# Exponent rows of the next head pair made behind the eighth score product of a pair, their copy behind the seventh exponential

## The reference

```python
q = einsum('bfd,dnh->bfnh', layernorm(x), wq) * 8 ** -0.5      # 16 heads of 8, 128 queries
k = einsum('btd,dnh->btnh', ctx, wk); v = einsum('btd,dnh->btnh', ctx, wv)   # 2048 keys
w = softmax(einsum('btnh,bfnh->bnft', k, q) + bias)            # over the keys
x = x + einsum('bfnh,nhd->bfd', einsum('bnft,btnh->bfnh', w, v), wo)
```

## Time and profile before

| what | value |
|---|---|
| median of 3 runs | 306.6 us (306.28 to 307.88) |
| the profiled execution | 306.75 us, its span 304.7 us |
| PE busy | 280.7 us (92%) |
| DVE busy | 228.3 us (75%) |
| ACT busy | 205.3 us (67%) |
| POOL busy | 70.9 us (23%) |
| mean granted TensorE clock | 0.989 of full speed |

### The profile page before, as it was taken

How to read it: one execution, slowest core, us unless ns; L and a number is a source line. 1 busy time by engine, 2 the same in 40 slices (tenths; PEclk the granted TensorE clock), 3 DMA queues, 4 the chain that set the end, 5 groups by cost and what they waited for, 6 DMA issues and landing times.

```text
span 304.7 us, 10417 instructions
## 1 busy us (share of the span) xinstructions
PE 280.7 (92%) x4400; PEld 181.5 (60%) x4404; DVE 228.3 (75%) x376; ACT 205.3 (67%) x419; POOL 70.9 (23%) x140
## 2 busy tenths in 40 slices
PE   7956999999989999889999899999899999999995
PEld 6544666666656665453656566666656666436575
DVE  5954889999799994474478999999799970753583
ACT  4647688988878987623454888988788987133350
POOL 6694510110110121421022865010010030020001
PEclk9995999999999999999999999999999999999999
DMA  7974414532212380233200036322222100000000
GB/s 244 406 256 134 162 55 169 193 89 87 71 54 76 91 295 2 105 140 106 68 1 0 5 89 227 126 85 67 73 72 59 54 3 4 0 2 2 0 0 17
DMA packets 10897, 28.11 MB, mean 92 GB/s; under 512 B 2241, under 2 KB 3329, under 8 KB 10466
## 3 DMA queue, kind: packets, MB, share of 16 engines
q1 hardware_dynamic: 10776, 27.22, 27.1%
q10 hardware_dynamic: 74, 0.20, 0.2%
HBM read 20.79 MB, written 6.62 MB: 90 GB/s over the span
## 4 chain that ended last, share of the span: by engine, by line
PE 59%; DVE 25%; ACT 5%; issue 3%; POOL 3%; DMA 3%; ACTq 1%; POOLq 0%; DVEq 0%
PE bank L1099 58%; DVE mx L852 15%; ACT probs L573 2%; DMA k_first_rows<-kparts 2%; DVE o_rec L809 1%; DMA kpair<-k_first_rows 1%; POOL m_rows L444 1%; DVE negm L859 1%; POOL m_rows L446 1%; DVE kparts L821 1%; DVE k_rest L818 1%; DVE s_neg L911 1%; DVE xn L779 1%; DVE st L760 1%; ACT o_all L500 1%
## 5 line engine op out<-in xcount | busy, mean ns | idle before, releaser
L852 DVE TENSOR_REDUCE mx<-bank 128x2 f32<-128x1024 f32 x128 | 152.7, 1221 | 15.9 <-PE bank L1099 13.3
L573 ACT ACTIVATE probs<-bank 128x512 f32<-128x512 f32 x256 | 139.8, 596 | 18.4 <-PE bank L1099 13.7
L1099 PE MATMUL bank<-q_exp,kpair 64*128 64x128 bf16 x1024 | 87.1, 218 | 1.6 <-ACT probs L573 1.2
L1099 PE MATMUL bank<-probs,v_all 128*9 128x128 f32 x2048 | 79.9, 274 | 1.6 <-ACT probs L573 1.4
L1099 PE MATMUL bank<-kpair,q_rows 64*128 64x512 bf16 x256 | 72.8, 386 | 5.6 <-DMA kpair<-k_first_rows 4.4
L1099 PEld LDWEIGHTS bank<-q_exp,kpair 64*128 64x128 bf16 x1024 | 56.0, 94 | 33.0 <-ACT probs L573 13.6
L1099 PEld LDWEIGHTS bank<-probs,v_all 128*9 128x9 f32 x2048 | 43.4, 90 | 18.0 <-ACT probs L573 4.3
L444 POOL CAST m_rows<-negm 128x2 bf16<-128x2 f32 x32 | 7.1, 221 | 136.6 <-DVE negm L859 136.6
L1099 PEld LDWEIGHTS bank<-kpair,q_rows 64*128 64x128 bf16 x256 | 22.4, 93 | 8.0 <-issue 4.8
L500 ACT ACTIVATE v_all<-bank 128x512 f32<-128x512 f32 (+1 forms) x20 | 10.5, 538 | 14.2 <-PE bank L1099 14.2
L374 POOL TENSOR_TENSOR y<-ve,mhalf 128x1 f32<-128x1 f32 (+1 forms) x10 | 5.8, 581 | 50.8 <-DVE ve L766 50.8
(11 more groups left out here) (224 smaller groups left out, 339.9 us busy)
## 6 DMA issues: line engine op xcount, KB each, us to landing
k_scratch<-kparts SPq DMA_DIRECT2D x24, 256.0 KB, 2.9
kpair<-k_scratch SPq DMA_DIRECT2D x62, 96.0 KB
kpair<-k_scratch SPq DMA_DIRECT2D x62, 64.0 KB
ctxT_s<-in_ctxT SPq DMA_DIRECT2D x4, 512.0 KB, 6.3
mask_s<-in_mask SPq DMA_DIRECT2D x2, 1024.0 KB, 11.2
kpair<-k_scratch SPq DMA_DIRECT2D x62, 32.0 KB
wM<-in_packM SPq DMA_DIRECT2D x1, 1728.0 KB, 7.1
wB<-in_packB SPq DMA_DIRECT2D x1, 654.0 KB, 5.0
```

Of the source, the lines that this page charges most:

```text
L573: act.activation(probs[:, j % 4, :], bank[:, 4 + j % 2, :], ACT.Exp).then_inc(S("exp_done"), 1)
L852: V.tensor_reduce(mx[n % 2][:, w, :], bank[:, 2 * (w % 2):2 * (w % 2) + 2, :], AX.X, ALU.max) \
L1099: return T.matmul(out_, lhsT=lhsT, rhs=rhs, start=start, stop=stop, **kw)
```

## The change

Two statements move. On PE, `put_exp(n + 1)` leaves its place ahead of step 3 (ahead of `b_unit(n, 6)`, the seventh score product) and stands behind `b_unit(n, 7)`, the eighth, ahead of `pv_group(n, 2)`. On ACT, `put_qe(n + 1)` stands behind the exponential of j = 6 instead of that of j = 5. Nothing is added or removed.

```diff
--- before.py
+++ after.py
@@ -627,7 +627,7 @@
                         if l == 0 and j == 3 and n < 2:
                             fold(n + 2)
-                        if j == 5 and n + 1 < NN:
+                        if j == 6 and n + 1 < NN:
                             put_qe(n + 1)
@@ -1358,14 +1358,14 @@
                 for n in range(NN):
                     for k in range(4):
                         an, aw = (n + 1, 2 + k) if k < 2 else (n + 2, k - 2)
-                        if k == 3 and n + 1 < NN:
-                            put_exp(n + 1)
                         b_unit(n, 2 * k)
                         if an < NN:
                             a_ready(an, aw)
                             a_head(an, aw, 1)
                             a_head(an, aw, 0).then_inc(S("a_done"), 1)
                         b_unit(n, 2 * k + 1)
+                        if k == 3 and n + 1 < NN:
+                            put_exp(n + 1)
                         if k == 1 and n == NP:
                             sums(0)
```

## The result

The changed kernel takes 305.5 us (median of 8 runs, 304.23 to 305.89) against 307.76 us (median of 8, 306.28 to 308.08) in the same comparison: ratio 0.9932, 95% interval 0.9907 to 0.9957. Run again beside other kernels it had the ratios 0.9955 (0.9937 to 0.9974) and 0.9918 (0.9889 to 0.9947). By all three intervals it is faster, by 2.1 us after the first ratio. I forecast 5.2 us (301.4 from 306.6) and a range that ended at 304.8.

What follows compares the result with a forecast made beforehand. PE's wait for `m_rows` at `put_exp` was taken to bound normal units; gains of 1.66 + 1.24 + 2.6 = 5.5 us gave 301.1, less 0.3 given back for DVE: 301.4 us, range 300.3 to 304.8.

Steps and rivals of the forecast that it cites:

- What bounded the kernel: In a normal unit, a ring from `put_exp` over PE, DVE's maximum, `negate` and POOL to the next `put_exp`: 5.33 us.
- The price of the copy on ACT: On ACT, behind the exponential of j = 6, the moved copy delays the next exponential by 0.17 us.
- the upper bound, 0.32: Highest price in us of the copy on ACT, taken as a rival: 304.4 us in all, chance 0.12.
- The 0.05 us beyond the stall: In a normal unit, `b_unit` 1 comes at 1.74 us against 1.79 before without stall, making the unit 5.07 us.
- R: The time at which PE is free for step 3, which begins with the seventh score product.
- units 4 and 8: Units that hang on the exponential of j = 0, left out of the eight gains of 0.05 us in units 1 to 8.
- Each `put_exp` so gains its stall and 0.05 us: Per unit, the wait for `m_rows` (0.21 us in a normal unit) goes and `b_unit` 1 comes 0.05 us earlier.
- The stretch bound by DVE: From the sums of unit 8 to the `negate` for unit 12, DVE has no gap; `put_exp(12)` stays 17.7 us behind.
- At its end PE and ACT stand better: After DVE's stretch, each layer gains 0.60 us at unit 12, then 0.56 and 0.15 in units 13 to 15.
- The sign in the chain: In normal units the profile's chain would pass ACT's exponential instead of `negm` and POOL.
- The second (DVE takes over): DVE keeps a unit from being shorter than 5.2 us: 3.0 us gained, 303.6 us, chance 0.15.
- the third: The stall only moves, to `put_exp`'s new place or `b_unit` 1's wait for the exponential: 306.6 us, chance 0.1.

Runs made afterwards that it cites:

- experiment 2: Kernel before with only the copy `put_qe` moved behind the exponential of j = 6, `put_exp` left in place: 311.63 us, ratio 1.0129.
- Experiment 4: Four idle products added in step 1 of nine units, in both kernels: 309.79 us (ratio 1.0098) before, 311.84 us (1.0167) changed.
- experiment 5: Changed kernel with `put_exp` ahead of the eighth product, behind the `a_head` products or directly behind the seventh product: 307.24 us (ratio 1.0002) and 307.27 us (1.0015).

## Why the prediction was wrong

The sign was right, and so was the wait that goes away; the size was 2.5 times too large and the range missed, since the gain was worked out on a kind of unit that is only part of the 30.

- *What bounded the kernel*: right for normal units. The ring through `m_rows` is gone from the waits, and the stall of 0.21 us with it. Normal units went from 5.33 to 5.12 us, so their stall was the gain. In most units with a side job the `m_rows` ring didn't bound: they were already on the ring of products and exponentials, 4.94 us and the side job.
- *The price of the copy on ACT*: right. 0.18 us measured for 0.17; the upper bound, 0.32, is excluded by experiment 2.
- *The 0.05 us beyond the stall*: not there. The prediction took it from `b_unit` 1, at R + 1.74; it came at 1.78, since the eighth product came at R + 0.31 and the exponent rows at 0.64 instead of 0.60. But an earlier `b_unit` 1 would have given nothing either: the ring passes through `b_unit` 0, which the prediction itself had at R + 1.38, against 1.39 before. It applied this to units 4 and 8 only.
- **The step that failed** is "Each `put_exp` so gains its stall and 0.05 us". I worked out one normal unit and used it for all. In it the eighth product waits for ACT only until R + 0.31, nearly nothing, because `b_unit` 5 had waited before and made PE late. In a unit with a side job `b_unit` 5 doesn't wait, PE arrives earlier at step 3, and the eighth product waits until R + 0.46 for the exponential of j = 5. Before, `put_exp` stood in that gap and cost nothing: in the old order, with the rows there, it filled 0.22 us in which the eighth product couldn't start anyway. Behind the eighth product nothing covers it: it lengthens the way to the next unit's first product from 0.93 to 1.10 us, and the ring from 4.94 to 5.12. Such a unit lost 0.1 to 0.2 us instead of gaining 0.05 (unit 13 alone gained 0.19, as its stall of 0.37 us for POOL's slow cast, 0.58 us in place of 0.19, went away). In layer 1 that took nearly all that its units up to 8 had gained (0.26 for 1.24).
- *Side jobs lose their shadow.* In a normal unit of the kernel before the ring passed from step 1's `a_head` to DVE, beside the place of the side jobs; the new one passes through that place. Experiment 4 measures the difference: 0.15 of a 0.54 us load in the old kernel, 0.54 of it in the new.
- *The stretch bound by DVE*: its length was right. From `o_rec` to the `negate` for unit 12 it is 99.56 - 82.64 = 16.92 us after, 100.00 - 83.08 = 16.92 before. "At its end PE and ACT stand better" was too large, for the same reason: `put_exp(12)` started at 100.57, when the rows had been there since 100.26, because the eighth product ahead of it waited until 100.25 for ACT. `b_unit` 1 (1.14 behind it after, 1.79 before) comes 102.55 - 101.71 = 0.84 earlier, of which 0.44 had been won before: 0.40 instead of 0.60. The units 12 to 14 then lost 0.20 together (16.62 for 16.42) instead of gaining 0.7.
- *The sign in the chain*: not seen. The prediction wanted the chain of normal units to pass ACT's exponential. The profile's chain for the changed kernel stays on PE through all of them, for the waits for ACT there are short gaps between products; that ACT is on the ring is read from the distances above, not from the chain.

```profile
59.11 19.00 PE bank L1099 x365
```

- *The rivals*: none was the case. The second (DVE takes over) put units at 5.2 for a reason that didn't apply (they last 5.12); the third was half of it: what PE saved went, in some units, into a wait of the eighth product for the exponential, not of `b_unit` 1.

## What to carry to other kernels

When work leaves one ring, write down the next one, product by product, before pricing the gain: here it stood at 4.94 us under the old one of 5.33, and the very piece that moved lengthened it to 5.12. That has to be worked out for each kind of unit, not for the normal one: the place that is free in a unit where PE is late can be on the path in a unit where it is early. Look also at what the old ring hid. Work that ran beside the old wait comes back in full when that wait is gone, and a small dummy load in both kernels shows it in two runs.

## What the runs showed of the hardware

*Half-array products in pairs.* A full-array pair of products (`put_exp`) costs 0.22 us between steps and 0.54 us between half-array products that otherwise run side by side (experiment 5). The Trainium skill, "TensorEngine Tiling (Array Packing)", section Key Properties, says that a change of the tiling mode drains TensorE. The rows agree in that the exponent rows start 0.33 us behind the start of the seventh `b_unit`, while the eighth one starts 0.24 us behind the seventh where both are half-array products and nothing is waited for (66.30 to 66.53). How much of the 0.54 is a drain and how much the missing partner isn't told apart here.

*The beginning.* The first `put_exp` came between 32.57 and 36.42 us in the profiled executions, ahead of anything that the kernels differ in. The window 20 to 40 us, the kernel before and then the same with load (two views):

```profile
20.00:40.00 20.00, 14.84 (x138) 10.38 (x136) 12.34 (x13) 12.60 (x27) 10.13 (x15) 0.83 0.42 134
```

```profile
20.00:40.00 20.00, 13.01 (x90) 8.92 (x92) 10.64 (x11) 10.83 (x22) 9.51 (x13) 0.74 0.41 135
```

The column before the last two is the clock as a share of the full 2.4 GHz. At two levels, full and half, 0.83 is 6.8 us at 1.2 GHz and 0.74 is 10.4 us. Within the window PE idled for the first rows of keys, 4.4 us in the kernel before and 4.6 in the loaded one, until 25.27 us in both. The first `put_exp` came at 33.55 and 35.81 us: the longer stretch at the low level goes with a start 2.3 us later, as much as the change is worth. It isn't set by the change: executions with mean clocks of 0.983 and of 0.989 occur for one and the same kernel, before and after. Nor is it all of the spread. With 0.989 alone, the kernel before took 305.91 to 308.54 us beside the repetition of the changed kernel; what moves those executions stays open.
